# One-hot rows of a mixture-of-experts router laid out token and choice innermost, in bf16, with three moves in the queues

## The reference

```
x = layernorm(x + attention(x))              # 16 heads of 128, full softmax
scores = sigmoid(x @ router_w.T)             # 32 experts, in 8 groups of 4
sc = scores + e_bias
keep the 3 groups with the largest sum of their two best sc
topk_idx = the 4 best experts of a token; topk_w = scores there / their sum * 2.5
every expert has C = 160 slots; the (token, choice) pairs are sorted by expert,
    pos = rank of a pair within its expert, and pairs with pos >= C are dropped
out[token] += (silu(x Wg) * (x Wu)) Wd * topk_w     # over the filled slots
shared = silu(x Sg) * (x Su) @ Sd            # all tokens, 512 hidden features
x = layernorm(x + out + shared)
```

## Time and profile before

| | us |
|---|---|
| median of 3 runs (2802.04 to 2803.43) | 2802.78 |
| the profiled execution's own time | 2804.82 |
| its span, first to last instruction | 2803.1 |
| PE busy in the span | 2755.0 |
| DVE busy | 2185.9 |
| ACT busy | 1405.3 |
| POOL busy | 637.9 |

### The profile page before, as it was taken

The page is one execution under the profiler, slowest core; times in us unless marked ns, Lnnn a source line. Parts: engine busy times, 40 slices in busy tenths (PEclk is TensorE's granted clock), DMA queues, the critical chain, the costliest instruction groups (busy, mean ns, idle before and its releaser), DMA issues.

```text
span 2803.1 us, 41819 instructions
## 1 busy us (share of the span) xinstructions
PE 2755.0 (98%) x13088; PEld 2287.4 (82%) x13088; DVE 2185.9 (78%) x3194; ACT 1405.3 (50%) x2495; POOL 637.9 (23%) x627
## 2 busy tenths in 40 slices
PE   8999999999999999999999999999999999999988
PEld 7888888888888888888888888888887878888867
DVE  5888888888888888888888888888888777433346
ACT  5555555566555555755555556555555321244424
POOL 2121211122222122221111213221211100266510
PEclk9999999999999999999999999999999889999999
DMA  3111111113111111221111113111110411478943
GB/s 117 38 35 38 34 37 34 34 34 116 34 37 35 34 34 38 64 84 37 34 34 34 34 36 110 34 37 34 34 42 27 138 48 41 136 229 252 246 135 138
DMA packets 209640, 193.53 MB, mean 69 GB/s; under 512 B 14620, under 2 KB 162076, under 8 KB 209552
## 3 DMA queue, kind: packets, MB, share of 16 engines
q1 hardware_dynamic: 199056, 180.47, 20.4%
q0 software_dynamic: 10496, 12.02, 2.2%
HBM read 166.41 MB, written 36.18 MB: 72 GB/s over the span
## 4 chain that ended last, share of the span: by engine, by line
PE 89%; DVE 4%; DMA 3%; issue 2%; ACT 1%; POOL 1%; SPq 0%; POOLq 0%; ACTq 0%; DVEq 0%
PE banks L1718 36%; PE banks L1733 24%; PE banks L1756 12%; PE banks L1640 4%; PE banks L1689 3%; PE banks L1649 3%; DMA acc_rows<-rows_b,who 2%; PE banks L1702 2%; PE banks L1743 2%; PE banks L1571 1%; DVE colsum L1277 0%; POOL acc_rows L686 0%; PE banks L1676 0%; PE banks L1596 0%; DVE neg_max L1262 0%
## 5 line engine op out<-in xcount | busy, mean ns | idle before, releaser
L1718 PE MATMUL banks<-xt,w_sb 128*128 (+1 forms) x4608 | 1108.6, 390 | 6.6 <-DVE xt L1356 6.5
L906 ACT ACTIVATE rows_a<-banks,neg_max 128x1024 f32<-128x1024 f32 x512 | 572.5, 1118 | 893.2 <-DVE neg_max L1262 892.8
L1718 PEld LDWEIGHTS banks<-xt,w_sb 128*128 128x128 f32 x4608 | 866.3, 188 | 187.2 <-POOL w_sb L625 6.5
L1262 DVE TENSOR_REDUCE neg_max<-banks 128x1 f32<-128x1024 f32 x512 | 626.0, 1223 | 285.9 <-PE banks L1733 283.1
L1733 PE MATMUL banks<-qk 128*128 128x512 f32 x3072 | 781.0, 390 | 3.2 <-ACT rows_a L906 3.0
L1733 PEld LDWEIGHTS banks<-qk 128*128 128x128 f32 x3072 | 576.9, 188 | 124.8 <-issue 3.4
L1277 DVE SCALAR_TENSOR_TENSOR colsum<-rows_a,inv,colsum 128x1024 f32<-128x1024 f32 x448 | 586.3, 1309 | 18.8 <-DVE inv L1269 1.5
L625 POOL TENSOR_TENSOR w_sb<-raws,w_sb 128x512 fp32r<-128x512 f32 x192 | 258.0, 1344 | 1201.6 <-ACT w_sb L860 1201.6
L1756 PE MATMUL banks<-wo_sb,val 128*128 128x512 f32 x1536 | 372.0, 391 | 1.2 <-DVE y_sb L1312 1.2
L1756 PEld LDWEIGHTS banks<-wo_sb,val 128*128 128x128 f32 x1536 | 285.9, 188 | 67.8 <-DVE y_sb L1312 8.0
L1640 PE MATMUL banks<-xt 128*128 128x512 f32 x768 | 194.7, 413 | 0.0
(11 more groups left out here) (184 smaller groups left out, 2262.5 us busy)
## 6 DMA issues: line engine op xcount, KB each, us to landing
raws<-in_w_qkv SPq DMA_DIRECT2D x192, 256.0 KB, 2.9
wo_raw<-in_w_o SPq DMA_DIRECT2D x64, 256.0 KB, 2.8
y_sb<-in_x SPq DMA_DIRECT2D x32, 256.0 KB, 4.2
raw_own<-in_w_gate SPq DMA_DIRECT2D x16, 512.0 KB
raw_own<-in_w_up SPq DMA_DIRECT2D x16, 512.0 KB
raw_own<-in_w_down SPq DMA_DIRECT2D x16, 512.0 KB
raws<-in_xT SPq DMA_DIRECT2D x25, 256.0 KB, 3.0
x_wide<-y_sb SPq DMA_DIRECT2D x24, 256.0 KB, 3.7
```

What stands on the lines that cost most here:

```text
L906: act.activation(ex[:, t % 2], p_s[:, t % 2], ACT.Exp, bias=neg_max[:, t % 2], accum_out=rowsum[:, t % 2]).then_inc(act_e, 1)
L1262: dve.tensor_reduce(neg_max[:, t % 2], p_s[:, t % 2], AX_X, ALU.max, negate=True)\
L1718: ins = pe.matmul(p_g[:, g % 2], w_sb[:, a, r, c], xt_part(batch_par, b, c, half * NB, NB), start=(c == 0 and (a, b) == PASSES[0]), stop=( ...
```

## The change

All of the one-hot tensors are bf16 and hold the 16 (tile, choice) pairs innermost: `hot` is [expert, tile, choice], `named_hot` [part, expert, pair], `place_hot` [slot, pair]. They are compared with whole index arrays of the same shape (`iota_ei`, 512 elements, and `iota_s`, 2560 elements, where there were 32 and 160 that were broadcast), and `ei` and `pos_k` are first copied to bf16. `tmp` keeps its f32 layout and reads `hot` across it. `fill` reads both tensors with a step of 16 elements, 32 bytes. `scale_x(6)` and `scale_x(7)` move from VectorE to POOL; on SP `load_rows(5)` is issued ahead of `store_x(7)`; on VectorE `stats_o(0)` goes behind `share_step(5, 1)` and `lo_t(3, 0..1)`. `exT` moves out of the place that it had in memory, so two ACT statistics write their unused output elsewhere.

```diff
-        place_hot = sb("place_hot", [P, TT * TOPK, C_SLOTS], BF16, of=table_ctx)
-        named_hot = sb("named_hot", [P, TT * TOPK, 2, E], BF16, of=table_ctx)
+        place_hot = sb("place_hot", [P, C_SLOTS, TT * TOPK], BF16, of=table_ctx)
+        named_hot = sb("named_hot", [P, 2, E, TT * TOPK], BF16, of=table_ctx)
+        iota_s = sb("iota_s", [P, C_SLOTS, TT * TOPK], BF16, of=table_ctx)
...
-    iota_s = sb("iota_s", [P, C_SLOTS])
-    names = sb("names", [P, TURNS * TT * TOPK, 2])
+    iota_ei = sb("iota_ei", [P, E, TT * TOPK], BF16)
+    names = sb("names", [P, 2, TURNS * TT * TOPK], BF16)
+    unused_row = sb("unused_row", [P, D], BF16)
+    ei_b = sb("ei_b", [P, TT, TOPK], BF16)
+    pos_b = sb("pos_b", [P, TT, TOPK], BF16)
...
-    hot = sb("hot", [P, TT, TOPK, E], BF16)
+    hot = sb("hot", [P, E, TT, TOPK], BF16)
...
         load_rows(4)
-        store_x(7)
         sp.wait_ge(pe_t, TT * 4)
         load_rows(5)
+        store_x(7)
         store_a(2)
...
+        on_pool.wait_ge(pe_o, T * PAIRS)
+        pool.iota(iota_ei[:], [[1, E], [0, TT * TOPK]], base=0, channel_multiplier=0,
+                  allow_small_or_imprecise_dtypes=True).then_inc(pool_k, 1)
...
-        pool.iota(iota_s[:], [[1, C_SLOTS]], base=0, channel_multiplier=0,
+        pool.iota(iota_s[:], [[1, C_SLOTS], [0, TT * TOPK]], base=0, channel_multiplier=0,
...
+        scale_x(6)
         for c in range(TURNS):
             on_pool.wait_ge(dve_w, 2 * c + 2)
             pool.dma_start(rows_of(weights_of, c), dense[:, c % 2]).then_inc(out_w[c % 2], 16)
+            if c == 1:
+                scale_x(7)
...
-            ro.step(tt(hot[:], ei[:, :, 0:TOPK].unsqueeze(3).to_broadcast([P, TT, TOPK, E]),
-                       iota_e[:].unsqueeze(1).unsqueeze(1).to_broadcast([P, TT, TOPK, E]), ALU.is_equal))
-            ro.step(dve.tensor_reduce(chosen[:], hot[:].rearrange("p t k e -> p t e k"), AX_X, ALU.max))
+            on_dve.wait_ge(pool_k, 1)
+            ro.step(dve.tensor_copy(ei_b[:], ei[:, :, 0:TOPK]))
+            ro.step(tt(hot[:].rearrange("p e t k -> p e (t k)"),
+                       ei_b[:].rearrange("p t k -> p (t k)").unsqueeze(1).to_broadcast([P, E, TT * TOPK]),
+                       iota_ei[:], ALU.is_equal))
+            ro.step(dve.tensor_reduce(chosen[:].rearrange("p t e -> p e t"), hot[:], AX_X, ALU.max))
...
-            tt(named_hot[:], hot[:].rearrange("p t k e -> p (t k) e").unsqueeze(2)
-               .to_broadcast([P, TT * TOPK, 2, E]),
-               names[:, i].unsqueeze(3).to_broadcast([P, TT * TOPK, 2, E]), ALU.mult).then_inc(dve_e, 1)
+            tt(named_hot[:], hot[:].rearrange("p e t k -> p e (t k)").unsqueeze(1)
+               .to_broadcast([P, 2, E, TT * TOPK]),
+               names[:, :, i].unsqueeze(2).to_broadcast([P, 2, E, TT * TOPK]), ALU.mult).then_inc(dve_e, 1)
...
-            ro.step(tt(tmp[:], hot[:], pos[:].unsqueeze(2).to_broadcast([P, TT, TOPK, E]), ALU.mult))
+            ro.step(tt(tmp[:], hot[:].rearrange("p e t k -> p t k e"), pos[:].unsqueeze(2).to_broadcast([P, TT, TOPK, E]), ALU.mult))
             ro.step(dve.tensor_reduce(pos_k[:], tmp[:], AX_X, ALU.add))
-            tt(place_hot[:], pos_k[:].rearrange("p t k -> p (t k)").unsqueeze(2)
-               .to_broadcast([P, TT * TOPK, C_SLOTS]),
-               iota_s[:].unsqueeze(1).to_broadcast([P, TT * TOPK, C_SLOTS]), ALU.is_equal).then_inc(dve_e, 1)
+            ro.step(dve.tensor_copy(pos_b[:], pos_k[:]))
+            tt(place_hot[:], pos_b[:].rearrange("p t k -> p (t k)").unsqueeze(1)
+               .to_broadcast([P, C_SLOTS, TT * TOPK]), iota_s[:], ALU.is_equal).then_inc(dve_e, 1)
...
-        scale_x(6)
         weigh(0)
...
             collect(u)
-            if u == 2:
-                scale_x(7)
...
         share_step(5, 0)
-        stats_o(0)
         share_step(5, 1)
         lo_t(3, 0, True)
         lo_t(3, 1, True)
+        stats_o(0)
         share_step(5, 2)
...
-                    ins = pe.matmul(p_k[:, h].rearrange("p v e -> p (v e)"), place_hot[:, i, h * HALF:(h + 1) * HALF],
-                                    named_hot[:, i].rearrange("p v e -> p (v e)"),
+                    ins = pe.matmul(p_k[:, h].rearrange("p v e -> p (v e)"), place_hot[:, h * HALF:(h + 1) * HALF, i],
+                                    named_hot[:, :, :, i].rearrange("p v e -> p (v e)"),
```

More of the change, by code:

```diff
@@ L226, in layer @@
     xT_flat = sb("xT_flat", [P, TT * D])
[L227 removed]
     with ExitStack() as table_ctx:
[L229 to L230 removed]
+        place_hot = sb("place_hot", [P, C_SLOTS, TT * TOPK], BF16, of=table_ctx)
+        named_hot = sb("named_hot", [P, 2, E, TT * TOPK], BF16, of=table_ctx)
+        iota_s = sb("iota_s", [P, C_SLOTS, TT * TOPK], BF16, of=table_ctx)
         dense = sb("dense", [P, 2, TT, E], of=table_ctx)
         tmp = sb("tmp", [P, TT, TOPK, E], of=table_ctx)
+    exT = sb("exT", [P, 2, KC, C_SLOTS])
     ehb = sb("ehb", [P, 2, 2, EC * C_SLOTS], F32R)
@@ L715, in _ @@
                                ALU.subtract).then_inc(pool_s, 1)
-        pool.iota(iota_s[:], [[1, C_SLOTS]], base=0, channel_multiplier=0,
+        pool.iota(iota_s[:], [[1, C_SLOTS], [0, TT * TOPK]], base=0, channel_multiplier=0,
                   allow_small_or_imprecise_dtypes=True).then_inc(pool_k, 1)
-        pool.iota(names[:, :, 0], [[0, TURNS * TT * TOPK]], base=1, channel_multiplier=1,
+        pool.iota(names[:, 0], [[0, TURNS * TT * TOPK]], base=1, channel_multiplier=1,
                   allow_small_or_imprecise_dtypes=True).then_inc(pool_k, 1)
-        pool.iota(names[:, :, 1].rearrange("p (t k) -> p t k", k=TOPK), [[1, TURNS * TT], [0, TOPK]], base=0,
+        pool.iota(names[:, 1].rearrange("p (t k) -> p t k", k=TOPK), [[1, TURNS * TT], [0, TOPK]], base=0,
                   channel_multiplier=0, allow_small_or_imprecise_dtypes=True).then_inc(pool_k, 1)
+        scale_x(6)
         for c in range(TURNS):
@@ L755, in read_x @@
                 on_act.wait_ge(act_q, 2 * (TT * c + j))
-                unused = rows_c[:, 0] if c < 6 else exT[:].rearrange("p q k s -> p (q k s)")[:, 0:D]
+                unused = rows_c[:, 0] if c < 6 else unused_row[:]
                 act.activation(unused, rows, ACT.Identity, scale=-1.0 / D,
@@ L1083, in _ @@
         link = Chain(dve, ln_c)
[L1085 to L1089, removed]
         def stats_o(c, tiles=range(TT)):
@@ L1187, in place @@
             on_dve.wait_ge(pe_k, c)
-            on_dve.wait_ge(pool_k, 3)
-            tt(named_hot[:], hot[:].rearrange("p t k e -> p (t k) e").unsqueeze(2)
-               .to_broadcast([P, TT * TOPK, 2, E]),
-               names[:, i].unsqueeze(3).to_broadcast([P, TT * TOPK, 2, E]), ALU.mult).then_inc(dve_e, 1)
+            on_dve.wait_ge(pool_k, 4)
+            tt(named_hot[:], hot[:].rearrange("p e t k -> p e (t k)").unsqueeze(1)
+               .to_broadcast([P, 2, E, TT * TOPK]),
+               names[:, :, i].unsqueeze(2).to_broadcast([P, 2, E, TT * TOPK]), ALU.mult).then_inc(dve_e, 1)
             on_dve.wait_ge(pe_c, c + 1)
```

## The result

| | before | after |
|---|---|---|
| median of 4 runs, us | 2802.41 | 2826.69 (2823.57 to 2833.75) |
| ratio, 95% interval | | 1.0095 [1.0071, 1.0120] |
| profiled execution, us | 2804.82 | 2826.91 |
| its span, us | 2803.1 | 2825.1 |
| PE busy / DVE busy, us | 2755.0 / 2185.9 | 2798.6 / 2168.8 |

The change makes the kernel 24.3 us slower; 2795.6 was forecast, in a range that ended at 2812. VectorE does less, as it should. TensorE does more.

The account below looks back on a forecast made before the run. The prediction took TensorE as the bound, with the gain in its waits. Terms -5.2 -2.9 -9.7 +10.6 sum to -7.2 us, from a median of 2802.8 to 2795.6 us; range 2783 to 2812.

Parts of the forecast that it names:

- What bounds the kernel: Routing and last stage: TensorE is the bound, so the gain lies in its waits, not in VectorE's busy time.
- VectorE's arithmetic: Routing on VectorE: 1.7 us less per turn, shortening TensorE's waits at count(1), the transposes and count(6); term -2.9 us.
- the half slope for bf16: VectorE's one-hot compares: all-bf16 adjacent operands halve time per element; named_hot 1.22 to 0.68, place_hot 2.82 to 1.49 us.
- What it costs on TensorE: Eight fills reading at 32-byte steps: 54 ns more a pair, +1.7 us a fill, partly covered by waits; term +10.6 us.
- the second rival: Fills become the bound: 139 ns a pair, +3.2 us a fill, three more slow gate_ups +5; 2811.7 us, chance 0.25.
- the slow stretch behind the load's wait: TensorE after its wait for load_rows(5), clock at 0.50: 1.5 us won back, bounds 0 and 2.6.
- Cover and the load: TensorE's 3.72 us load wait goes, term -5.2 us; waits at fill(0), fill(1), fill(5) cover 2.5, 0.8, 0.6 us.
- Roots on POOL: scale_x(6) and scale_x(7) in routing: 4.8 us each on POOL, nothing waits; term 0.
- Late statistics: Last stage: TensorE's 9.40 us hole goes, a new 2.0 us wait comes before down(5); term -9.7 us.
- Free hops: Rival at the fills: stepped reads cost TensorE nothing, the fill term goes; 2785.0 us, chance 0.22.
- no doubling: Rival on VectorE: bf16 doesn't double the rate, the -2.9 becomes about +1; 2799.5 us, chance 0.07.
- a moving tail wait: Rival in the last stage: late rows or stats_o(2) make down(5) start 5 us later than forecast; 2800 us, chance 0.06.

Follow-up runs that it names:

- experiment 4: The changed kernel with fill reading adjacent, wrong elements and its results zeroed; routing ends at 2416.41 us, 0.02 off the kernel with only the three queue edits (2416.43).
- experiment 7: The kernel before with one edit, stats_o(0) called after the two lo_t(3, ...) calls: 2788.61 us, ratio 0.9963.
- experiment 3: The three queue edits with the old layout, plus extra matmuls at varied steps before each fill: at 32 bytes 146 ns a pair (weights), 118 (moving data), 150 (both).
- Experiment 5: The kernel with only the three queue edits, each fill issued four times over with adjacent operands: 2808.83 us, ratio to before 1.0039.
- experiment 2: The changed kernel with the three queue edits undone, so the new layout alone: 2834.46 us, ratio 1.0148.
- experiment 9: The kernel before with only scale_x(6) and scale_x(7) moved to POOL: 2789.53 us, ratio 0.9974.
- experiment 6: The changed kernel with place_hot back in the old order and arithmetic, so only the moving data hops: 2813.2 us in one run.

## Why the prediction was wrong

**What bounds the kernel, and VectorE's arithmetic: right, and of no use.** TensorE was the bound, the half slope for bf16 was right to within 10 ns (chosen at 752 ns and tmp at 1095 were each some 60 ns over what was taken for them), and at count(1) and the late transposes the waits shrank by 1.0 and 1.2 us, as worked out (-1.2, -1.3). But experiment 4 shows no earlier end from it where -2.9 was forecast. The two ends of routing differ by 0.02 us, which puts the term at nothing; but it is one profile of each, and two profiles of the same instructions ended routing 4.5 us apart (experiment 7), so a gain of 2.9 us isn't excluded. In the changed kernel the waits are covered by the fills anyway.

**What it costs on TensorE: the step that failed.** I took 0.67 ns as the surcharge of a hop for "the nearest row", VectorE's, and so 92 ns a pair. It measured 148. The error isn't only one of size. A surcharge is added to an engine's pace; what the fills show is a pace of its own, 1.8 ns a column, that takes the place of TensorE's and doesn't follow its clock (experiment 3). VectorE's whole 1.74 ns, which I had as the upper bound, is close to it, and so is tmp's in the changed kernel, (1095 - 147) / 512 = 1.85 ns. That the two engines meet one limit of the memory is suggested by these figures and not shown. The bound was the better price, and my own argument in the second rival said so ("the memory, not the engine, sets it"). The fills' term becomes 28.2 instead of 13.7 before cover: 14.5 us.

**The clock: the larger miss.** The forecast put nothing for the clock behind slower fills and took -1.5 us for the slow stretch behind the load's wait; the second rival gave three slow gate_ups, +5. Measured was +19.3. The rival had the mechanism, but counted it for a few places; the clock fell behind all eight fills. Experiment 5 shows that it isn't their length that brings it. With hops 45.0 us of routing are lost (experiment 4): 28.2 by the fills, 21.6 by other work at a lower clock, less 4.8 of waits.

**Cover and the load: half right.** The 3.72 us of waiting went, but the layout alone has only 0.18 of it left (experiment 2), so the term of -5.2 was already eaten by the fills. Cover all told was 10.9 us of idle time, where waits removed and cover together came to 9.7 in the sum (3.72 + 2.9 + 3.1).

**Roots on POOL: no cost, as said.** POOL's iota of 2560 elements took 3.05 us and scale_x(6) ended at 2209.4, 2 us sooner than worked out. What I overlooked is that the store behind it, and so the load behind the store, would have been early by this edit alone (experiment 9). I had written that ACT writes at 2273 instead of 2284 and didn't follow it on to SP's queue.

**Late statistics: right, too small.** The last stage lost 12.5 us, not 9.7. The new wait of 2.0 us in front of down(5) didn't come, since the rows were there almost when VectorE asked (0.56 us of wait), and gate_up(5, 3) took 5.73 us where before it had run behind the hole in 7.75. That the rows were there is partly luck: their last scatter-add was issued 8.1 us behind gate_up(5, 0), and 12.2 in the execution on which the forecast was worked out. The medians give late statistics 10.4 us alone (experiment 7).

**The account.** -7.2 forecast, +14.5 fills, +20.8 clock (19.3 and the 1.5 that was not won), -1.2 more idle time gone (10.9 against 9.7), -2.8 tail, -2.1 in the experts' stage: +22.0, the difference of the spans. The last is chance: the experts took 254.0 us before and 252.0 in experiment 7, with the same instructions. By the same token the clock's part can be off by some 4 us.

**The rivals.** Of the second, 139 ns a pair was close and 2811.7 was 15 us short, most of it clock. Free hops, no doubling and a moving tail wait are ruled out by the profile.

## What to carry to other kernels

When a layout makes a writer cheaper, price its readers first: here some 1.6 us a turn on VectorE (the five durations fell by 2.0, the two copies took 0.4), mostly hidden, was bought with 3.5 us a turn on TensorE, which was the bound. If an engine's price for an access pattern isn't in the trace, give another engine's whole time per element a fair chance and not only its surcharge; here the whole time was nearly right, in one case. Profile the kernel before more than once before forecasting its waits: two profiles of the same instructions differed by 4.5 us at the end of routing. And sum queue edits only after asking whether they mend the same wait; take them on their own: the kernel with those three edits alone is the fastest here, 2781.6 to 2782.8 us.

## What the runs showed of the hardware

- A bf16 operand of TensorE read with a step of 16 or 32 bytes takes 1.8 ns per column, as weights or as moving data, at granted clock 1.00 and 0.50 alike (weights 143 and 146 ns a pair, moving data 118 in experiment 6 at 1.00 and 118 in experiment 3 at 0.50); 8 bytes take 0.93 ns, 4 bytes nothing beyond the 38 ns of an adjacent pair. Load and product still overlap.
- Behind such fills the clock is low although TensorE counts as busy all the time: 0.84 to 1.00 within the eight fills, and 0.50 for the 7 us behind one. The same 4.9 us filled with adjacent pairs stayed at 1.00.
- On VectorE tmp, which now hops by 32 bytes, went from 684 to 1095 ns for 512 elements, 0.8 ns each; chosen, which no longer hops, went from 1036 to 752 ns.
- POOL's iota of 2560 bf16 elements took 3.05 us, 1.2 ns each.
